# Layer 3 of a graph network: keys and values gathered together, values kept in DRAM in item order

## Chip, cores and metric

The kernel runs on one core of a Trainium2 chip. The time is device microseconds of one execution. Three runs of the kernel before gave 3381.06, 3384.52 and 3429.43 us; the median is 3384.52 us. An engine is named as in the profile: PE is TensorE (PEld its weight loads), DVE VectorE, ACT ScalarE, POOL GpSimd and SP SyncE, which here only issues transfers.

## The reference

Three graph layers run one after the other over 3125 nodes of 256 numbers and 50,000 edges sorted by their destination: two attention convolutions (8 heads, then 1), and one layer of query, key and value attention with 4 heads of 64. Only the third is touched by the change:

```
Q = (enh @ Wq + bq);  K = (enh @ Wk + bk);  V = (enh @ Wv + bv)      # enh = x + 0.1 * query_emb
scores = sum_d Q[dst] * (K[src] + 0.2 * rel[type]) / 8               # per edge and head
w   = exp(scores - max over dst) / (sum over dst)
agg = segment_sum(w * V[src], dst);  msgs = agg where a node has edges, else V
out = layernorm(x + layernorm(msgs @ Wo + bo + x) * gamma + beta)
```

So each edge needs two rows of its source node, one of K for the score and, once all scores are known, one of V for the sum.

## The kernel before

The nodes lie in 25 blocks of 128. The edges are cut into 416 **items** (`ITEMS`): up to 128 edges, one per partition, all of whose destinations lie in one block. Eight items are a **group** (`GROUP`), so there are 52 groups; four groups (`SLOTS`) are a turn (`TURNS` is 13). All engines follow one written program, stage by stage: node1, score1, sum1, node2, score2, soft2, sum2, node3, score3, soft3, sum3, final. A stage begins when the engines it names have ended the one before (`begin`, L345). Otherwise engines meet only in semaphores.

**node3** (`node3_products` L1071, `kv_copies` L1234) makes Q, K and V block by block. Q goes to `query`, a view of the second half of `row_space` in SBUF. K and V go through `stage` to the DRAM tables `tab_k` and `tab_v` with 256 numbers per row, two stores per block (`store`, L502).

**Gathers.** POOL fetches rows by index (`gathers`, L693). One indirect DMA fetches one row for each of the 128 edges of an item, 1 KB each, so a group takes eight of them into one slot (`row_slots`, L165). The pass for K (n = 2) has a ring of four slots, because `query` takes the rest of the space; the pass for V (n = 3) has eight (`RINGS`, L49). Before it fills a slot POOL waits until DVE has read what was in it (`slot_used`, L718). The V pass starts once the K pass is issued, takes its first four slots as they come free, and the other four once PE has ended score3 (L715).

**score3** (`pair_scores` L847 on PE, L1245 on ACT, L1562 on DVE; `score_rows` L526 on SP). For each group SP broadcasts two rows of small numbers to all partitions (types, destinations; 128 KB each as written, in pieces of 1 KB). ACT makes one-hot matrices of them, PE multiplies these with the relations and with Q of the block in two halves of four items, and tells with `pair_mm` that a half is done. DVE waits for the group's K rows and for the half, adds (L1580), multiplies (L1588) and reduces (L1570). ACT's next one-hots wait for `pair_mm` too.

**soft3** normalises the scores with a scan over all edges (L1616).

**sum3** (`sums`, L905 on PE, L1176 on ACT, L1668 on DVE). Per group DVE waits until PE has used the buffer two groups back (`sum_mm`, L1682), builds the one-hot of destinations (L1683), waits for the V rows, weighs them (L1688) and copies the shares (L1692). PE adds the eight items into the PSUM bank of their block (L918) and tells `sum_mm`; ACT moves each full block to `acc` (L1195), which waits for `sum_mm` as well. The same functions make sum2, with rows of layer 2.

**final** reads V back (`load_v`, L497) and makes the output.

`acc` holds the sums of a layer; node3 is the last to read those of layer 2, and sum3 writes it next.

Of the kernel before, what the change touches and what calls it, by code (L numbers as in the profile page):

```python
# [48 lines left out]
RINGS = [2 * SLOTS, 2 * SLOTS, SLOTS, 2 * SLOTS]  # L49
BTURNS = BLOCKS // UB  # L50
# [46 lines left out]
def graph_layers(nc, a, out):  # L97
    ctx = ExitStack()
    with ctx:
# [12 lines left out]
        tab_k = dram("tab_k", (NP, D))  # L112
        tab_v = dram("tab_v", (NP, D))
# [37 lines left out]
        query = query_space[:, 0:BLOCKS * D].rearrange("p (b d) -> p b d", b=BLOCKS)  # L151
# [158 lines left out]
        gathered = [sem(f"rows_gathered{s}") for s in range(2 * SLOTS)]  # L310

# [105 lines left out]
        def _(sp):  # L417
# [79 lines left out]
            def load_v(t, j):  # L497
                if not early(t, j, UB):
                    sp.wait_ge(x_used, nth_block(t, j, 1, 1 - UB))
                sp.dma_start(stage[:, j, 1], tab_v[bass.ds((t * UB + j) * P, P), :]).then_inc(x_loaded[j], 16)  # L500
# [25 lines left out]
            def score_rows(layer, name, first):  # L526
# [7 lines left out]
                with nc.sync.Fori(0, TURNS) as u:  # L534
                    for s in range(SLOTS):

                        sp.wait_ge(onehot_made[s % 2], nth(u, s) + (layer * HALF + 1))
                        for k in range(2):
                            row = flat[k][bass.ds(u * (STEP * P // 2) + s * GROUP * P // 2, GROUP * P // 2)]
                            sp.dma_start(bcast_words[:, s % 2, k], row.partition_broadcast(P)).then_inc(bcast_in[s % 2], 16)  # L540
                end()
# [63 lines left out]
            seg_rows("soft3", H3, P // H3)  # L605

# [20 lines left out]
            stored(5 * BTURNS)  # L627

        @block.gpsimd
        def _(pool):  # L630
# [62 lines left out]
            def gathers(n, table, name):  # L693

                ring, turns, rest = RINGS[n], (GROUPS - 1) // RINGS[n], (GROUPS - 1) % RINGS[n] + 1
                pool.wait_ge(phase["sp"], STAGES.index(name) + 1)

                def indices(u, s):

                    for k in (s, s + 1):  # L700

                        pool.wait_ge(gathered[k], u * (16 * GROUP) + (uses(n, k) * 16 * GROUP))
                    nc.gpsimd.tensor_copy(  # L703
                        index_slot[:, s:s + 2].rearrange("p s g -> p (s g)"),
                        src_i[:, bass.ds(u * (ring * GROUP) + s * GROUP, 2 * GROUP)]).then_inc(pool_step, 1)

                def gather(u, s, ends):
# [12 lines left out]
                    pool.sem_inc(slot_claimed, 1)  # L720
                    for g in range(GROUP):
                        nc.gpsimd.indirect_dma_start(  # L722
                            (wide_rows[:, s] if n == 0 else row_slots[s])[:, g, :], None, table,
                            bass.IndirectOffsetOnAxis(ap=index_slot[:, s, g:g + 1], axis=0),
                        ).then_inc(gathered[s], 16)

                indices(0, 0)
                with nc.gpsimd.Fori(0, turns) as u:
                    for s in range(ring):
                        gather(u, s, False)  # L730
                for s in range(rest):
                    gather(turns, s, s + 1 == rest)
                step.add(GROUPS // 2)
# [3 lines left out]
            gathers(2, tab_k, "node3")  # L737
            gathers(3, tab_v, "node3")
# [365 lines left out]
        def _(act):  # L1104
# [129 lines left out]
            def kv_copies(t, j):  # L1234
                act.wait_ge(node_mm, nth_block(t, j, 2, 1))
                act.wait_ge(node_stored[j], t * 32 + 16 * 2 * BTURNS)
# [40 lines left out]
        def _(dve):  # L1277
# [284 lines left out]
            def pair_scores(layer, name):  # L1562
# [10 lines left out]
                def multiply(u, s, reduce_before):  # L1573
# [3 lines left out]
                    for half in range(2):  # L1577
# [4 lines left out]
                            rows[:, s, items, :].rearrange("p i (h d) -> p i h d", h=H3),  # L1582
# [85 lines left out]
            def sums(n, name, heads, width, nth_pass):  # L1668
# [7 lines left out]
                def build(u, s):  # L1676
# [10 lines left out]
                    dve.wait_ge(gathered[s], u * (16 * GROUP) + ((uses(nth_pass, s) + 1) * 16 * GROUP))  # L1687
# [400 lines left out]
            def final_iteration(t, j):  # L2088
# [63 lines left out]
                if outer_too:  # L2152
                    after(1)

                    dve.wait_ge(node_stored[jd], td * 16 + 16 * 4 * BTURNS)
# [50 lines left out]
```

## Time and profile before

| | us |
|---|---|
| median of three runs | 3384.52 (3381.06 to 3429.43) |
| span of the profiled execution | 3410.9 |
| of it score3, about 1958 to 2645 | 687 |
| soft3, 2645 to 2697 | 52 |
| sum3, 2697 to 3295 | 598 |
| busy PE / DVE / POOL / ACT, whole span | 1633.6 / 1540.5 / 1641.8 / 406.0 |

The profile gives the profiled execution's span alone and no further time around it; 3410.9 us is 26.4 us above the median of the runs and inside their spread. No engine is busy for even half of the span: POOL and PE 48%, DVE 45%. The page's chain of work that ended last puts 36% down to "another core or an unknown queue". The queue of POOL's gathers moved 219.91 MB and took 22.7% of what 16 DMA engines have, SP's queue 69.66 MB and 8.1%. A busy share is an average over stages with different limits, so it has to be read stage by stage.

### The profile page before, as it was taken

Reading aid. Unit: us, or ns where it says so; the run is one execution under the profiler, and the core shown is the slowest. Engines: PE = TensorE matmul, PEld = TensorE weight load, DVE = VectorE, ACT = ScalarE, POOL = GpSimd, SP = SyncE. Lnnn points to the kernel's source line nnn. Section 1 sums busy time; section 2 is a strip of 40 time slices with the busy share of each in tenths; the row PEclk is TensorE's granted clock in tenths of the full one; section 3 lists DMA queues with packets and bytes.
Section 4 is the critical chain, followed back from the end, with each engine's and each line's share of the span. In section 5 each row is a group of like instructions: output and inputs, shape, how many; then the busy total and the mean of one; then the engine's idle time right before and its main releaser. Section 6 shows DMA issues by size and latency. Waiting matters only on the chain.

```text
span 3410.9 us, 30471 instructions
## 1 busy us (share of the span) xinstructions
PE 1633.6 (48%) x7573; PEld 1176.0 (34%) x7574; DVE 1540.5 (45%) x2386; ACT 406.0 (12%) x809; POOL 1641.8 (48%) x1791
## 2 busy tenths in 40 slices
PE   3624334335367342443345945655566233333455
PEld 2313323223255332332233434444344222322343
DVE  3225454536464772232235535545565432322368
ACT  0100000000012000000001433333333100000012
POOL 0240656455502715655660065665656756556600
PEclk8855767667688556766667967777777566666765
DMA  1532323223303522322321343343333323223211
GB/s 33 125 92 55 86 70 92 63 82 82 80 29 99 165 77 83 91 82 82 89 85 34 98 115 98 104 106 98 105 99 102 99 79 91 82 82 89 85 29 61
DMA packets 166449, 289.97 MB, mean 85 GB/s; under 512 B 37842, under 2 KB 113035, under 8 KB 166411
## 3 DMA queue, kind: packets, MB, share of 16 engines
q0 software_dynamic: 79872, 219.91, 22.7%
q1 hardware_dynamic: 86539, 69.66, 8.1%
q14 instruction: 27, 0.22, 0.0%
q8 instruction: 11, 0.18, 0.0%
HBM read 272.74 MB, written 16.68 MB: 85 GB/s over the span
## 4 chain that ended last, share of the span: by engine, by line
another core or an unknown queue 36%; DVE 23%; PE 21%; issue 13%; DMA 4%; DVEq 1%; SPq 1%; ACT 0%; POOL 0%; ACTq 0%; POOLq 0%
PE ps L918 5%; DVE arena L1688 5%; PE ps L870 3%; DMA arena<-rows_block_dst 3%; DVE arena L1931 2%; PE ps L1077 2%; DVE arena L1580 2%; DVE scores L1570 2%; DVE arena L1588 1%; PE ps L797 1%; PE ps L1054 1%; PE ps L1003 1%; DVE arena L1924 1%; DVE arena L1498 1%
## 5 line engine op out<-in xcount | busy, mean ns | idle before, releaser
L722 POOL DMA_INDIRECT row_space<-tab_feat,index_slot x832 | 816.5, 981 | 687.4 <-issue 322.5
L918 PE MATMUL ps<-arena 128*128 128x257 f32 (+1 forms) x1664 | 481.9, 457 | 702.2 <-DVE arena L1692 504.8
L918 PEld LDWEIGHTS ps<-arena 128*128 128x128 f32 x1664 | 379.3, 233 | 804.7 <-issue 731.6
L722 POOL DMA_INDIRECT row_space<-tab_k,index_slot x416 | 393.9, 947 | 255.8 <-issue 162.1
L722 POOL DMA_INDIRECT row_space<-tab_v,index_slot x416 | 403.4, 970 | 229.1 <-issue 128.4
L1683 DVE TENSOR_TENSOR arena<-ps,block_dst 128x1024 f32<-128x1024 f32 x104 | 127.0, 1222 | 809.0 <-remote 681.9
L1003 PE MATMUL ps<-arena 128*128 128x265 f32 x832 | 249.8, 463 | 102.8 <-DVE ps L1914 49.5
L870 PE MATMUL ps<-row_space,arena 128*128 x832 | 294.0, 514 | 0.0
L1580 DVE TENSOR_TENSOR arena<-row_space,ps 128x1024 f32<-128x1024 f32 x104 | 126.8, 1219 | 322.0 <-remote 223.7
L1195 ACT COPY acc<-ps 128x265 f32<-128x265 f32 (+2 forms) x75 | 28.2, 376 | 1786.8 <-remote 1064.6
L1003 PEld LDWEIGHTS ps<-arena 128*128 128x128 f32 x832 | 189.1, 233 | 149.0 <-issue 107.9
L1688 DVE TENSOR_TENSOR arena<-row_space,ps 128x2048 f32<-128x2048 f32 x104 | 236.8, 2277 | 0.0
L703 POOL COPY index_slot<-src_i 128x16 int32 (+1 forms) x104 | 23.8, 229 | 432.8 <-SPq L419 432.5
L864 PE MATMUL ps<-rel_stack,arena 128*128 128x64 bf16 x416 | 92.4, 222 | 275.1 <-DVE arena L1588 159.8
L870 PEld LDWEIGHTS ps<-row_space,arena 128*128 128x128 f32 x832 | 202.1, 255 | 40.0
L864 PEld LDWEIGHTS ps<-rel_stack,arena 128*128 128x128 bf16 x416 | 43.1, 104 | 322.8 <-DVE arena L1588 179.2
L1588 DVE TENSOR_TENSOR arena<-arena,ps 128x1024 f32<-128x1024 f32 x104 | 127.0, 1221 | 9.6 <-DVE arena L1580 3.7
L1570 DVE TENSOR_REDUCE scores<-arena 128x2048 f32 (+1 forms) x52 | 118.5, 2280 | 0.0
L1931 DVE TENSOR_TENSOR arena<-row_space,ps 128x2048 f32<-128x2048 f32 x52 | 118.3, 2276 | 0.0
L950 PE MATMUL ps<-er_parts,arena 128*128 x416 | 56.4, 199 | 127.7 <-issue 74.5
L1253 ACT ACTIVATE arena<-arena,minus_type_no 128x1024 bf16<-128x1024 uint8 x52 | 59.7, 1148 | 446.1 <-remote 332.4
L836 PE MATMUL ps<-el_parts,arena 128*128 128x25 bf16 x1248 | 62.0, 183 | 89.1 <-DVE arena L1498 72.3
(316 smaller groups left out, 2120.1 us busy)
## 6 DMA issues: line engine op xcount, KB each, us to landing
arena<-rows_block_dst SPq DMA_DIRECT2D x156, 128.0 KB
row_space<-tab_feat,index_slot POOLq DMA_INDIRECT x832
arena<-rows_src_low SPq DMA_DIRECT2D x52, 128.0 KB
arena<-rows_type SPq DMA_DIRECT2D x52, 128.0 KB
row_space<-tab_k,index_slot POOLq DMA_INDIRECT x416
row_space<-tab_v,index_slot POOLq DMA_INDIRECT x416
arena<-in_x_t SPq DMA_DIRECT2D x50, 128.0 KB, 2.2
tab_feat<-arena SPq DMA_DIRECT2D x25, 132.0 KB, 1.8
```

The costliest lines, as they stand in the source:

```text
L722: nc.gpsimd.indirect_dma_start((wide_rows[:, s] if n == 0 else row_slots[s])[:, g, :], None, table, bass.IndirectOffsetOnAxis(ap=index_slo ...
L864: nc.tensor.matmul(relation, type_onehot[:, s % 2, e], rel_stack[:, 0, :], start=True, stop=False)
L870: last = nc.tensor.matmul(ps[:, bank, at:at + D], query_onehot[:, s % 2, g * P:(g + 1) * P], query[:, bass.ds(bs[g], 1), :].rearrange("p a ...
L918: last = nc.tensor.matmul(ps[:, SUM_BANKS:2 * SUM_BANKS][:, bass.ds(bs[g], 1), 0:width].rearrange("p a d -> p (a d)"), onehot[:, s % 2, g, ...
L1003: last = nc.tensor.matmul(ps[:, SUM_BANKS:2 * SUM_BANKS][:, bass.ds(banks[s % 2 * GROUP + g], 1), 0:AW].rearrange("p a d -> p (a d)"), one ...
L1077: nc.tensor.matmul(at, h_t[:, j, k, :], w_a[:, k, w0:w1], start=k == 0, stop=False)
L1570: vec.tensor_reduce(by_item(H3)[:, bass.ds(u * STEP + s * GROUP, GROUP), :], pair_product[:, s % 2].rearrange("p i (h d) -> p i h d", h=H3 ...
L1580: then(vec.tensor_tensor(pair_product[:, z, items, :].rearrange("p i (h d) -> p i h d", h=H3), rows[:, s, items, :].rearrange("p i (h d) - ...
L1588: vec.tensor_tensor(pair_product[:, z, items, :], pair_product[:, z, items, :], ps[:, 2 * half:2 * half + 2, :].rearrange("p q (i d) -> p ...
L1683: vec.tensor_tensor(onehot[:, z], ps[:, SHARE_BANK:SHARE_BANK + 1, IOTA_AT:IOTA_AT + P].broadcast_to([P, GROUP, P]), block_dst[:, bass.ds( ...
L1688: vec.tensor_tensor(weighted[:, z, :, 0:D].rearrange("p i (h d) -> p i h d", h=heads), row_slots[s].rearrange("p i (h d) -> p i h d", h=he ...
L1931: vec.tensor_tensor(weighted[:, z, :, 0:D].rearrange("p i (h d) -> p i h d", h=H1), wide_rows[:, half * SLOTS + g, :, 0:D].rearrange("p i ...
```

## The change

- node3 stores K and V of a block as one row of 512 numbers in `tab_kv`, in one store per block.
- Q no longer lies in `row_space` but in `acc`, so that four slots of double width fit (`kv_rows`).
- The K pass gathers from `tab_kv`: as many indirect DMAs as before, with rows of 2 KB. Before it fills a slot again POOL also waits for `values_stored`.
- In score3 SP stores the value half of each group, once gathered, in `item_v`, a DRAM tensor in item order (1 MB per group). It issues that after the next group's broadcasts.
- The V pass of gathers is gone. SP loads the groups of `item_v` plainly into eight slots, the first eight after it has issued soft3's rows, the others in sum3 as DVE frees the slots. DVE waits for `values_in`.

The diff, cut to its core:

```diff
+PREFETCH = 2 * SLOTS
-        tab_k = dram("tab_k", (NP, D))
-        tab_v = dram("tab_v", (NP, D))
+        tab_kv = dram("tab_kv", (NP, 2 * D))
+        item_v = dram("item_v", (GROUPS, P, GROUP * D))
-        query = query_space[:, 0:BLOCKS * D].rearrange("p (b d) -> p b d", b=BLOCKS)
+        kv_rows = row_space[:, 0:SLOTS * GROUP * 2 * D].rearrange("p (s g d) -> p s g d", s=SLOTS, g=GROUP)
+        query = acc[:, :, 0:D]
...
+            def store_values(u, s):
+                sp.wait_ge(gathered[s], u * (16 * GROUP) + (uses(2, s) + 1) * 16 * GROUP)
+                sp.dma_start(item_v[bass.ds(u * SLOTS + s, 1)].rearrange("a p (g d) -> (a p) g d", g=GROUP),
+                             kv_rows[:, s, :, D:2 * D]).then_inc(values_stored[s], 16)
+
+            def load_values(u, s):
+                sp.wait_ge(slot_used[s], u + (uses(3, s) + 1))
+                sp.dma_start(row_slots[s].rearrange("p g d -> p (g d)"),
+                             item_v[bass.ds(u * PREFETCH + s, 1)].rearrange("a p d -> (a p) d")).then_inc(values_in[s], 16)
...
+                else:
+                    spread(0, 0)
+                    with nc.sync.Fori(0, TURNS - 1) as u:
+                        for s in range(SLOTS):
+                            spread(u + (s + 1) // SLOTS, (s + 1) % SLOTS)
+                            keep(u, s)
...
-            pipeline(nc.sync.Fori, [(0, load_x), (4, store(2, tab_k, tab_v))])
-            stored(4 * BTURNS)
+            def store_kv(t, j):
+                sp.wait_ge(node_act, nth_block(t, j, 2, 1))
+                sp.dma_start(tab_kv[bass.ds((t * UB + j) * P, P), :],
+                             stage[:, j].rearrange("p a d -> p (a d)")).then_inc(node_stored[j], 16)
+            pipeline(nc.sync.Fori, [(0, load_x), (4, store_kv)])
...
-            score_rows(2, "score3", "type")
+            score_rows(2, "score3", "type", keep=store_values)
             seg_rows("soft3", H3, P // H3)
+            for s in range(SLOTS):
+                sp.wait_ge(values_stored[s], 16 * TURNS)
+            for s in range(PREFETCH):
+                load_values(0, s)
             begin(sp, "sum3", ["dve", "pe", "act"])
...
+            with nc.sync.Fori(0, GROUPS // PREFETCH - 1) as u:
+                for s in range(PREFETCH):
+                    load_values(u + 1, s)
+            for s in range(GROUPS % PREFETCH):
+                load_values(GROUPS // PREFETCH, s)
...
-                    if n == 3 and s == SLOTS:
-                        pool.wait_ge(phase["pe"], STAGES.index("score3") + 1)
                     pool.wait_ge(slot_used[s], u + (uses(n, s) + 1))
+                    if kept:
+                        pool.wait_ge(values_stored[s], u * 16)
...
-            gathers(2, tab_k, "node3")
-            gathers(3, tab_v, "node3")
+            gathers(2, tab_kv, "node3")
...
-                            rows[:, s, items, :].rearrange("p i (h d) -> p i h d", h=H3),
+                            kv_rows[:, s, items, 0:D].rearrange("p i (h d) -> p i h d", h=H3),
...
-                    dve.wait_ge(gathered[s], u * (16 * GROUP) + ((uses(nth_pass, s) + 1) * 16 * GROUP))
+                    if nth_pass == 3:
+                        dve.wait_ge(values_in[s], u * 16 + 16)
+                    else:
+                        dve.wait_ge(gathered[s], u * (16 * GROUP) + ((uses(nth_pass, s) + 1) * 16 * GROUP))
```

`spread` is the old body of SP's loop, the two broadcasts of one group.

## Rows read from the trace of the kernel before

**Rows 1.** Busy time of the engines by stretch, with PEclk, DMA share and GB/s.
```profile
core 0: us, PE busy (x) PEld busy (x) DVE busy (x) ACT busy (x) POOL busy (x), PEclk, DMA share, GB/s
1112.00:1180.00 68.00, 28.01 (x736) 25.86 (x736) 52.48 (x94) 0.00 (x0) 56.34 (x43) 0.50 0.61 168
1845.00:1935.00 90.00, 76.44 (x241) 35.30 (x241) 59.58 (x181) 35.31 (x124) 0.00 (x0) 0.89 0.29 90
1958.00:2645.00 687.00, 409.80 (x1664) 285.62 (x1664) 362.05 (x257) 227.37 (x208) 420.46 (x466) 0.71 0.39 103
2645.00:2697.00 52.00, 8.96 (x38) 7.06 (x38) 26.75 (x39) 10.89 (x19) 38.32 (x33) 0.53 0.32 91
2697.00:3295.00 598.00, 240.09 (x832) 188.29 (x832) 183.68 (x165) 17.68 (x46) 348.63 (x386) 0.70 0.28 80
3256.00:3292.00 36.00, 31.62 (x128) 25.44 (x128) 27.07 (x25) 4.58 (x12) 0.00 (x0) 0.89 0.00 0
```

**Rows 2.** Groups of instructions in the sum stage of layer 3, 2697 to 3295 us.
```profile
L722 POOL DMA_INDIRECT row_space<-tab_v,index_slot x364 | 344.6, 947 | 204.2 <-issue 112.9 <-DVE arena L1688 89.5 <-POOL index_slot L703 1.8
L1688 DVE TENSOR_TENSOR arena<-row_space,ps 128x2048 f32<-128x2048 f32 x52 | 118.4, 2277 | 0.0
L1683 DVE TENSOR_TENSOR arena<-ps,block_dst 128x1024 f32<-128x1024 f32 x52 | 63.5, 1222 | 412.1 <-remote 359.9 <-PE ps L918 41.2 <-issue 8.4
```

**Rows 3.** Timeline of one cycle of four groups in that stage (start, duration).
```profile
2962.39 0.94 POOL L722 DMA_INDIRECT row_space<-tab_v,index_slot  x1 [9.54 <-DVE arena L1688]
...
2972.09 3.77 PE L918 MATMUL ps<-arena 128*128 128x260 f32 x16 [0.41 <-DVE arena L1692]
...
3001.34 0.95 POOL L722 DMA_INDIRECT row_space<-tab_v,index_slot  x1 [0.30 <-issue]
...
3007.53 0.38 ACT L1195 COPY acc<-ps 128x260 f32<-128x260 f32 x1 [40.93 <-remote]
3007.64 1.22 DVE L1683 TENSOR_TENSOR arena<-ps,block_dst 128x1024 f32<-128x1024 f32 x1 [23.85 <-remote]
```

**Rows 4.** Timeline of its last groups, after the last gather.
```profile
3272.81 1.22 DVE L1683 TENSOR_TENSOR arena<-ps,block_dst 128x1024 f32<-128x1024 f32 x1 [0.55 <-PE ps L918]
...
3276.58 7.28 PE L918 MATMUL ps<-arena 128*128 128x260 f32 x32 [0.30 <-DVE arena L1692]
...
3280.39 1.23 DVE L1683 TENSOR_TENSOR arena<-ps,block_dst 128x1024 f32<-128x1024 f32 x1 [0.55 <-PE ps L918]
...
3291.99 0.21 DVE L1704 TENSOR_SCALAR arena<-acc 128x100 f32<-128x100 f32 x1 [4.57 <-ACTq L1114]
```

**Rows 5.** Timeline of the score stage of layer 1, around its last prefetching gather.
```profile
207.25 0.36 DVE L1737 TENSOR_REDUCE scores<-ps 128x192 f32 x1 [20.05 <-remote]
...
223.23 0.95 POOL L722 DMA_INDIRECT row_space<-tab_feat,index_slot  x1 [0.30 <-issue]
...
228.94 0.36 DVE L1737 TENSOR_REDUCE scores<-ps 128x192 f32 x1 [20.67 <-remote]
```

**Rows 6.** Groups of instructions in the score stage of layer 3, 1958 to 2645 us.
```profile
L722 POOL DMA_INDIRECT row_space<-tab_k,index_slot x416 | 393.9, 947 | 255.8 <-issue 162.1 <-DVEq L1301 91.8 <-POOL index_slot L703 1.5
L1580 DVE TENSOR_TENSOR arena<-row_space,ps 128x1024 f32<-128x1024 f32 x103 | 125.6, 1219 | 316.0 <-remote 217.8 <-issue 65.9 <-PE ps L870 29.1
```

**Rows 7.** Timeline of one cycle of two groups in that stage.
```profile
2310.58 0.94 POOL L722 DMA_INDIRECT row_space<-tab_k,index_slot  x1 [6.07 <-DVEq L1301]
...
2328.41 1.22 DVE L1580 TENSOR_TENSOR arena<-row_space,ps 128x1024 f32<-128x1024 f32 x1 [9.66 <-remote]
...
2335.55 0.95 POOL L722 DMA_INDIRECT row_space<-tab_k,index_slot  x1 [5.19 <-issue]
...
2354.03 1.22 DVE L1580 TENSOR_TENSOR arena<-row_space,ps 128x1024 f32<-128x1024 f32 x1 [10.66 <-remote]
```

**Rows 8.** Stretches as in Rows 1: broadcasts alone; gathers and broadcasts together.
```profile
231.00:319.00 88.00, 46.15 (x340) 35.55 (x339) 44.94 (x87) 0.00 (x0) 0.00 (x0) 0.50 0.28 61
2346.00:2348.00 2.00, 1.11 (x3) 0.34 (x1) 0.00 (x0) 0.00 (x0) 1.51 (x2) 0.50 0.86 109
```

More of the change, by code:

```diff
@@ L310, in graph_layers @@
         gathered = [sem(f"rows_gathered{s}") for s in range(2 * SLOTS)]
+        values_stored = [sem(f"values_stored{s}") for s in range(SLOTS)]
+        values_in = [sem(f"values_loaded{s}") for s in range(2 * SLOTS)]
         slot_claimed = sem("rows_slot_claimed")
@@ L499, in load_v @@
                     sp.wait_ge(x_used, nth_block(t, j, 1, 1 - UB))
-                sp.dma_start(stage[:, j, 1], tab_v[bass.ds((t * UB + j) * P, P), :]).then_inc(x_loaded[j], 16)
+                sp.dma_start(stage[:, j, 1], tab_kv[bass.ds((t * UB + j) * P, P), D:2 * D]).then_inc(x_loaded[j], 16)
             def store(stage_no, *tables):
@@ L524, in _, with score_rows @@
             end()
-            def score_rows(layer, name, first):
+            def store_values(u, s):
[6 more added lines that the diff above has]
+                             item_v[bass.ds(u * PREFETCH + s, 1)].rearrange("a p d -> (a p) d")).then_inc(values_in[s], 16)
+            def score_rows(layer, name, first, keep=None):
                 begin(sp, name, ["dve", "pe", "act"])
@@ L533, in score_rows, with spread @@
                 flat = [rows_d[x].rearrange("i e -> (i e)") for x in (first, "block_dst")]
-                with nc.sync.Fori(0, TURNS) as u:
+                def spread(u, s):
+                    sp.wait_ge(onehot_made[s % 2], nth(u, s) + (layer * HALF + 1))
+                    for k in range(2):
+                        row = flat[k][bass.ds(u * (STEP * P // 2) + s * GROUP * P // 2, GROUP * P // 2)]
+                        sp.dma_start(bcast_words[:, s % 2, k], row.partition_broadcast(P)).then_inc(bcast_in[s % 2], 16)
+                if keep is None:
+                    with nc.sync.Fori(0, TURNS) as u:
+                        for s in range(SLOTS):
+                            spread(u, s)
+                else:
[4 more added lines that the diff above has]
+                            keep(u, s)
                     for s in range(SLOTS):
[L537 to L540, printed above, removed]
+                        if s + 1 < SLOTS:
+                            spread(TURNS - 1, s + 1)
+                        keep(TURNS - 1, s)
                 end()
@@ L600, in _ @@
                 sp.dma_start(bias_parts[k:k + 1, :], bias_split[:, k]).then_inc(bias_in, 16)
-            pipeline(nc.sync.Fori, [(0, load_x), (4, store(2, tab_k, tab_v))])
-            stored(4 * BTURNS)
+            def store_kv(t, j):
[3 more added lines that the diff above has]
+            pipeline(nc.sync.Fori, [(0, load_x), (4, store_kv)])
+            stored(3 * BTURNS)
             end()
-            score_rows(2, "score3", "type")
+            score_rows(2, "score3", "type", keep=store_values)
             seg_rows("soft3", H3, P // H3)
+            for s in range(SLOTS):
+                sp.wait_ge(values_stored[s], 16 * TURNS)
+            for s in range(PREFETCH):
+                load_values(0, s)
             begin(sp, "sum3", ["dve", "pe", "act"])
@@ L626, in _ @@
             pipeline(nc.sync.Fori, [(0, load_v), (5, store_out)])
-            stored(5 * BTURNS)
+            stored(4 * BTURNS)
         @block.gpsimd
@@ L705, in indices, with gather @@
                         src_i[:, bass.ds(u * (ring * GROUP) + s * GROUP, 2 * GROUP)]).then_inc(pool_step, 1)
-                def gather(u, s, ends):
+                rows_of_slot = {0: lambda s: wide_rows[:, s], 1: lambda s: row_slots[s], 2: lambda s: kv_rows[:, s]}[n]
+                def gather(u, s, ends, kept=False):
                     if s % 2 == 0:
@@ L727, in gathers @@
                 indices(0, 0)
-                with nc.gpsimd.Fori(0, turns) as u:
+                if n == 2:
                     for s in range(ring):
-                        gather(u, s, False)
+                        gather(0, s, False)
+                    with nc.gpsimd.Fori(0, turns - 1) as u:
+                        for s in range(ring):
+                            gather(u + 1, s, False, True)
+                else:
+                    with nc.gpsimd.Fori(0, turns) as u:
+                        for s in range(ring):
+                            gather(u, s, False)
                 for s in range(rest):
-                    gather(turns, s, s + 1 == rest)
+                    gather(turns, s, s + 1 == rest, n == 2)
                 step.add(GROUPS // 2)
@@ L1235, in kv_copies @@
                 act.wait_ge(node_mm, nth_block(t, j, 2, 1))
-                act.wait_ge(node_stored[j], t * 32 + 16 * 2 * BTURNS)
+                act.wait_ge(node_stored[j], t * 16 + 16 * 2 * BTURNS)
                 nc.scalar.copy(stage[:, j, 0, :], ps[:, product_bank(j), D:2 * D])
```

5 lines of the change are left out of this document (3 added, 2 removed).

## The prediction

> **What bounds the kernel now.** I read the page's slices first and saw no engine near full use, so I cut the span by stage [rows 1]. In sum3 (2697 to 3295 us) PE is busy 240 of 598 us, DVE 184, and the DMA engines carry 28% of what they can. POOL has 349 us of gathers, and with the gap after each of them they come every 1.25 us: eight per group and a copy of indices make about 10.1 us, so 52 groups cost POOL some 525 us. Next I read who waits in it: DVE never waits at the weighing that needs the rows (0.0 idle before L1688), but 412 us before the one-hot (L1683), 360 of them with an unknown releaser [rows 2]. By the program that instruction waits for PE's signal alone.
>
> The timeline shows what that is [rows 3]. POOL restarts at 2962.39 when DVE frees slots and issues four groups, 32 gathers, until 3002.29. PE finishes a group of matmuls at 2975.86 (2972.09 plus 3.77), yet ACT and DVE, who both wait for PE's count, move only at 3007.53 and 3007.64: 32 us after the matmuls and 5 us after POOL's last gather. The eight slots then free four again, and so on: 40 us of gathers plus 9.4 is the 49.4 us cycle. The rows themselves were there long before. Two more places bear out that PE's signals come late while POOL issues back to back, and not otherwise. At the end of sum3, with all gathers issued, two groups take 7.58 us (3272.81 to 3280.39), and PE's 7.28 us fill it [rows 4]. In score1, where DVE needs nothing gathered, its reductions stand at 207.25 and 228.94, and the second comes 4.8 us after POOL's last prefetch ended [rows 5]. In the stretch 1112 to 1180 of score2 it does not happen, though gathers and broadcasts move 168 GB/s: there the gathers are slower, 56.34 us for 43, 1.31 us each [rows 1]. I don't know the mechanism; the rows tie it to POOL issuing at full pace, not to bytes moved.
>
> Score3 is the same with four slots: POOL issues two groups (16 gathers, about 20 us), then waits about 5 us for DVE; it starts at 2310.58 and 2335.55, and DVE begins every second group 25.6 us apart [rows 7]. POOL's waits there are 256 us, DVE's 316 [rows 6].
>
> **The change, part by part.**
>
> Sum3 without POOL. The 416 gathers of V go. What is left per group is DVE's 1.22 + 2.28 us beside PE's 3.64 plus its gap, 3.79 in the steady pair [rows 2, 4]. From the start of the stage at 2697 [rows 1] to the first instruction of final at 3291.99 [rows 4] is now 595 us. After: 50 groups × 3.79 = 190, plus the 11.6 us from the one-hot of the last pair (3280.39) to that instruction, plus 3 us for PE starting at 1.2 GHz (granted clock 0.5) before it has 2.4: 204 us. **Gain 391 us.** ACT's copies of blocks already keep up at that pace in the last groups.
>
> The plain loads of V must feed this: 1.05 MB per 3.79 us is 277 GB/s. Eight groups are there before, since SP issues them during soft3 (52 us). The other 44 are 46.1 MB. No row shows 1 MB loads in pieces of 8 KB. Bounds: broadcasts alone carry 61 GB/s at a DMA share of 0.28 [rows 8], that is 218 GB/s, and 46.1 MB take 212 us; node loads and stores carry 90 GB/s at 0.29 [rows 1], 310 GB/s, and 149 us. With eight groups of lead 310 is ample, and 218 makes the stage about 15 us longer. I take no cost: long plain pieces should be nearer the node loads. SP's issues are cheap and in order, and only loads of weights stand ahead of them.
>
> Score3, gathers. The count is 416 as before, and POOL's pace per gather is that of descriptors, not bytes, as far as rows of 1 KB tell: no change of 10.1 us per group. But each moves 2 KB rows. Per pair of groups the DMA engines get 4.19 MB of gathers, 2.10 MB of stores of V and 0.52 MB of broadcasts. From rates at full share: gathers as in sum3, 80 GB/s at 0.28, 286 [rows 1]: 14.7 us. Stores as in node3, 310: 6.8 us. Broadcasts 218: 2.4 us. Sum 23.9 us in a cycle that now has 25.0 (POOL) to 25.6 (DVE). By score3's own mix, 103 GB/s at 0.39 = 264 GB/s, it is 25.8 us. So the stage moves from 39% to full DMA use. Ends: longer rows could be cheaper per byte, and then nothing changes (0); or the mix is dearer, as in the 2 us at 2346, 109 GB/s at a share of 0.86, 127 GB/s [rows 8], 54 us per pair. That end is two microseconds of one burst with small pieces in it, so I stay near the whole stage's mix and add 1 us for what queues at the burst's end: 26.8 us per pair, **24 pairs × 1.8 = +43 us**.
>
> Score3, the new waits. POOL waits also for the slot's store. A group is used by DVE some 30 us after its last gather (the group issued 2310.58 to 2320.3 starts at 2354.03 [rows 7]; its slot cannot be freed sooner). SP stores it when it has landed, a 1 MB store is 3.4 us at 310 GB/s, and even twice that ends long before: 0. If that cover went, the store's 3.4 us and the landing would come on each group. SP's order is the other risk: the store of group k stands before the broadcasts of k+2. Those are wanted only after PE has done group k, which needs DVE at k−1, while the rows of k have landed earlier: 0. ACT and DVE get no new instruction, and reading keys at double stride changes no shape.
>
> Score3's end. POOL's last gather of K is issued four groups before the end, and then the V pass fills the gap in the kernel before. Now POOL is silent, and the last four groups run at PE's 409.8/52 = 7.9 us instead of 687/52 = 13.2 [rows 1]: **−21 us**.
>
> Small edits, together: one 256 KB store instead of two per block in node3 (SP's issues lie beside PE's 76 of 90 us), Q copied to `acc`, the strided load in final: 0. Soft3: its chain is DVE, PE and ACT one after the other, and SP waits for the last stores behind soft3's rows, hidden by 52 us: 0.
>
> Sum: −391 + 43 − 21 = −369 us. Against the profiled 3410.9 us span that is 3042. The profiled execution stands 26.4 us above the median of the runs; carried to the median 3384.5 the forecast is **3015 us**.
>
> **A rule weighed.** The sum takes bytes at the rates of the rows. The Trainium skill, "DMA: Bandwidth & Descriptors", section Measured, lists 6.15 us for a transfer of 1 MB. By it 44 loads take 271 us, and sum3 would be bound by them; no run here shows a plain 1 MB load, and the rows' own lower bound is 218 GB/s. That speaks against this change, and stands below as rival C with its price from rows. The same page says transfers from all issuing engines interleave on the same 16 DMA engines, which the shares above assume and no row of mine separates.
>
> **Rivals.**
>
> A, 20%: score3's stall ends only when the gathers' queue has drained, not when POOL stops. For it: the release comes about 5 us after the last gather [rows 3, 5], time in which a queue could drain. Then the stores' 6.8 us per pair lie on the path, 31.8 instead of 25.0: 26 × 6.8 = 177, less the 21 of the end. Time 3384.5 − 391 + 156 = 3150.
>
> B, 8%: the opposite. Fuller DMA engines slow POOL's issue, as something does in score2 at 1.31 us per gather, and PE's signals come in time [rows 1]. Then score3 is bound by the DMA's 23.9 us per pair: 26 × 23.9 = 621 against 687. Time 3384.5 − 391 − 66 = 2928. Against it: the slowing in score2 goes with DVE's work there, which score3 does not have.
>
> C, 10%: loads bind sum3, which they do from below about 235 GB/s. At 218 GB/s the stage is 15 us longer; the dearest row I have, 127 GB/s [rows 8], makes it 165 longer. I price the middle, 172 GB/s: 268 us for the 44 loads, some 70 longer, time about 3085. Eight slots, and so several loads in flight, speak against it.
>
> D, 6%: signals come late under any heavy transfer, not POOL's. Four loads of 3.7 us and the 9.4 us of overhead of today's cycle [rows 3] give 24.2 us per four groups, 13 × 24.2 = 315 us for sum3. Time 3384.5 − 280 + 22 = 3126. Against it: the 168 GB/s of score2 without such stalls.
>
> E, 4%, slower than before: gathers, stores and broadcasts together fall to the 127 GB/s of the burst row [rows 8]. Then score3 takes 26 × 54 = 1400 us, 713 more, and the kernel 3384.5 − 391 + 713 = 3706. It decides from where a pair costs 25.0 + 391/26 = 40 us, 170 GB/s. The 168 GB/s of score2 at a share of only 0.61 speaks against that.
>
> **Numbers.** The forecast has 52%, with its own range 2960 to 3075. Predicted time 3015. The range 2930 to 3190 takes in A, C and D and half of B; outside it are E, the rest of B and the tails of A and C. A difference of 2%, 68 us, is about what a measurement of this kernel can tell from none. All cases but E lie far beyond it: faster 0.94, within 2% 0.02 (an A and a D together with dear stores), slower 0.04.
>
> **What would show it.** Right: no gathers in sum3, two groups of it about 7.6 us apart throughout, the stage near 205 us, PEclk near 1.0 in it; score3 at 680 to 740 us with a DMA share above 0.85 and POOL's 16 gathers still about 20 us long. Wrong: waits of DVE for `item_v` loads in sum3 (C); one-hots there with unknown releasers (D); POOL's pause in score3 grown from 5 to 12 us (A), or gone (B); gathers visibly longer than 1.25 us apart with the stage far over 750 us (E).

## The result, and the profile after

The changed kernel takes 3006.05 us (median of 4 runs, 2986.95 to 3031.9) against 3385.88 us before (median of 4 runs with one more taken beside it, 3381.06 to 3429.43): a ratio of 0.887, 95% interval 0.883 to 0.891. The forecast was 3015 us. The profiled execution, 3031.9 us, is the slowest of the four and counted as a slow run, while the ratio is of fast runs. Its span is 3030.2 us against 3410.9, 381 us less.

By stretch, in the profiled executions (us):

| | before | after | difference |
|---|---|---|---|
| start to the first gather of score3 | 1957.7 | 1963.0 | +5.3 |
| its 416 gathers, first to last | 654.0 | 676.3 | +22.3 |
| from the last gather to DVE's last product | 40.7 | 23.4 | −17.3 |
| from there over soft3 to the first one-hot of sum3 | 43.7 | 43.0 | −0.7 |
| sum3, to the first instruction of final | 595.9 | 205.3 | −390.6 |
| final | 118.9 | 119.2 | +0.3 |

The stretches after, to set beside [rows 1]: score3, soft3, sum3, the middle of sum3.

```profile
core 0: us, PE busy (x) PEld busy (x) DVE busy (x) ACT busy (x) POOL busy (x), PEclk, DMA share, GB/s
1963.00:2662.00 699.00, 398.20 (x1664) 279.81 (x1664) 363.13 (x259) 227.37 (x208) 399.10 (x441) 0.71 0.78 254
2662.00:2704.00 42.00, 8.95 (x38) 7.04 (x38) 24.06 (x37) 8.67 (x13) 0.00 (x0) 0.54 0.53 210
2704.00:2912.00 208.00, 190.93 (x832) 154.56 (x832) 183.63 (x158) 19.93 (x53) 0.00 (x0) 0.98 0.64 224
2720.00:2900.00 180.00, 170.69 (x752) 138.34 (x751) 164.36 (x141) 16.57 (x43) 0.00 (x0) 1.00 0.69 244
```

In sum3 POOL does nothing, PE is busy 191 of 208 us and its granted clock is 0.98 of full speed, where it was 0.70 in a stage in which PE was busy 240 of 598 us. The groups of that stage, beside [rows 2] (L1735 is the one-hot, L1743 the weighing):

```profile
L970 PE MATMUL ps<-arena 128*128 128x260 f32 x832 | 190.9, 387 | 19.8 <-DVE arena L1747 19.8
L1743 DVE TENSOR_TENSOR arena<-row_space,ps 128x2048 f32<-128x2048 f32 x52 | 118.4, 2277 | 0.0
L1735 DVE TENSOR_TENSOR arena<-ps,block_dst 128x1024 f32<-128x1024 f32 x52 | 63.7, 1224 | 20.7 <-PE ps L970 18.1 <-ACT ps L1233 2.6
```

DVE's wait before the one-hot fell from 412 to 21 us, and none of it has an unknown releaser ("remote") any more. The wait for the loaded values would stand before L1743; it is 0.0. The timeline of the steady stage, beside [rows 4]:

```profile
2799.63 1.22 DVE L1735 TENSOR_TENSOR arena<-ps,block_dst 128x1024 f32<-128x1024 f32 x1 [0.66 <-PE ps L970]
...
2803.14 1.23 DVE L1735 TENSOR_TENSOR arena<-ps,block_dst 128x1024 f32<-128x1024 f32 x1
...
2807.32 1.22 DVE L1735 TENSOR_TENSOR arena<-ps,block_dst 128x1024 f32<-128x1024 f32 x1 [0.66 <-PE ps L970]
```

Two groups take 7.69 us; without any transfer they took 7.58. The transfers of the values, from the page's list of DMA issues (count, KB each, median us from issue to landing where it has one):

```profile
item_v<-row_space SPq DMA_DIRECT2D x52, 1024.0 KB
row_space<-item_v SPq DMA_DIRECT2D x52, 1024.0 KB, 4.8
```

Score3, beside [rows 6] (L1632 is the product with the keys):

```profile
L768 POOL DMA_INDIRECT row_space<-tab_kv,index_slot x416 | 394.0, 947 | 278.0 <-issue 173.5 <-DVEq L1353 103.5 <-POOL index_slot L748 1.0
L1632 DVE TENSOR_TENSOR arena<-row_space,ps 128x1024 f32<-128x1024 f32 x104 | 126.7, 1219 | 327.4 <-remote 284.5 <-PE ps L922 23.0 <-issue 17.8
```

A gather of 2 KB rows costs POOL the same 947 ns as one of 1 KB rows. POOL waits 22 us more than before, DVE 11 us more, still mostly for an unknown releaser, and the DMA engines carry 254 GB/s at a share of 0.78 instead of 103 at 0.39. The gathers of a group take the same 9.80 us from the first issue to the end of the last, before and after; what grew is POOL's 24 pauses for a free slot, from 5.61 to 6.55 us on average, 22.6 us together.

The trace also records when a semaphore is raised, and that tells whose signal is late. From the end of a PE instruction that signals to the next recorded raise of its semaphore it takes 6.03 us in the median in this score3, where the same figure for DVE's and for ACT's signals is 0.01 us. In sum3 it was 6.74 us for PE before the change, up to 3240 us; it was 0.01 us there after the last gather, and it is 0.01 us after the change. (Where signals queue up the next raise can belong to an earlier one, and some raises are not recorded, so the figures of late signals are rough.)

### The profile page after: what moved, and what is told of

Same layout as the page of the kernel before. It is cut to its first block, busy times and chain, and to the rows that moved or that the text cites. A ratio compares the mean times of both kernels' runs of the same rounds, so it can differ in the third digit from the quotient of the medians.

```text
span 3030.2 us, 30129 instructions
## 1 busy us (share of the span) xinstructions
PE 1576.3 (52%) x7573; PEld 1138.0 (38%) x7574; DVE 1541.8 (51%) x2386; ACT 406.2 (13%) x809; POOL 1228.8 (41%) x1349
## 4 chain that ended last, share of the span: by engine, by line
another core or an unknown queue 28%; PE 27%; DVE 24%; issue 14%; DMA 5%; DVEq 1%; SPq 1%; ACT 0%; POOL 0%; ACTq 0%; POOLq 0%
PE ps L970 7%; DVE arena L1743 5%; PE ps L922 5%; DMA arena<-rows_block_dst 4%; PE ps L1129 2%; DVE arena L1986 2%; PE ps L1055 2%; DVE arena L1632 2%; PE ps L849 2%; PE ps L1106 1%; DVE scores L1622 1%; DVE arena L1979 1%; DVE arena L1640 1%; DVE arena L1550 1%
## 5 line engine op out<-in xcount | busy, mean ns | idle before, releaser
L970 PE MATMUL ps<-arena 128*128 128x257 f32 (+1 forms) x1664 | 427.4, 419 | 364.2 <-DVE arena L1747 305.7
L970 PEld LDWEIGHTS ps<-arena 128*128 128x128 f32 x1664 | 341.7, 210 | 449.9 <-issue 389.4
L768 POOL DMA_INDIRECT row_space<-tab_kv,index_slot x416 | 394.0, 947 | 278.0 <-issue 173.5
L1735 DVE TENSOR_TENSOR arena<-ps,block_dst 128x1024 f32<-128x1024 f32 x104 | 127.2, 1223 | 415.7 <-remote 327.9
L1632 DVE TENSOR_TENSOR arena<-row_space,ps 128x1024 f32<-128x1024 f32 x104 | 126.7, 1219 | 327.4 <-remote 284.5
L922 PE MATMUL ps<-acc,arena 128*128 x832 | 285.4, 502 | 0.0
L1055 PEld LDWEIGHTS ps<-arena 128*128 128x128 f32 x832 | 191.5, 236 | 149.6 <-issue 107.5
L1743 DVE TENSOR_TENSOR arena<-row_space,ps 128x2048 f32<-128x2048 f32 x104 | 236.8, 2277 | 0.0
L922 PEld LDWEIGHTS ps<-acc,arena 128*128 128x128 f32 x832 | 197.4, 249 | 38.6
L888 PEld LDWEIGHTS ps<-el_parts,arena 128*128 128x128 bf16 x1248 | 57.7, 108 | 105.1 <-issue 57.6
```

The costliest lines, as they stand in the source:

```text
L768: nc.gpsimd.indirect_dma_start(rows_of_slot(s)[:, g, :], None, table, bass.IndirectOffsetOnAxis(ap=index_slot[:, s, g:g + 1], axis=0),).th ...
L888: nc.tensor.matmul(ps[:, bank, at:at + w], onehot_t[:, s % 2, 0, e], el_parts[:, k, 0:w], start=k == 0, stop=k == 2)
L922: last = nc.tensor.matmul(ps[:, bank, at:at + D], query_onehot[:, s % 2, g * P:(g + 1) * P], query[:, bass.ds(bs[g], 1), :].rearrange("p a ...
L970: last = nc.tensor.matmul(ps[:, SUM_BANKS:2 * SUM_BANKS][:, bass.ds(bs[g], 1), 0:width].rearrange("p a d -> p (a d)"), onehot[:, s % 2, g, ...
L1055: last = nc.tensor.matmul(ps[:, SUM_BANKS:2 * SUM_BANKS][:, bass.ds(banks[s % 2 * GROUP + g], 1), 0:AW].rearrange("p a d -> p (a d)"), one ...
L1632: then(vec.tensor_tensor(pair_product[:, z, items, :].rearrange("p i (h d) -> p i h d", h=H3), kv_rows[:, s, items, 0:D].rearrange("p i (h ...
```

## The experiments

My theory: TensorE's signals to the other engines come late while POOL issues gathers at full pace. Sum3 was bound by that, and score3 still is. Against it: the stage was bound by the gathers' transfers, or by POOL's own time; and score3's 22 us could come from the longer rows or from the stores. Twelve runs were made, each beside the kernel before on its chip. Experiments 1 to 10 are one execution each. Experiments 1 to 4 ran on one chip, 5 to 10 on a second, 11 and 12 on a third (on which chip the result above was measured is not known); there the kernel before took 3441.6, 3441.6 to 3469.9, and 2809.7 us. Stages are compared within one chip where that can be done.

**1. Gathers nobody needs, in sum3.** The changed kernel, where POOL also issues 144 gathers:

```diff
             gathers(2, tab_kv, "node3")
+            for u in range(12):
+                for k in range(3):
+                    if u: pool.wait_ge(spare_in[k], u * 64)
+                    for g in range(4):
+                        nc.gpsimd.indirect_dma_start(spare[:, k, g, :], None, tab_feat2, ...).then_inc(spare_in[k], 16)
```

> The changed kernel, and in its sum3 POOL issues 144 gathers of layer 2's rows (1 KB each, about 180 us of issuing at 1.25 us each) into spare SBUF; nothing in the kernel waits for them but POOL itself. Theory (PE's signals come late while POOL issues back to back): as in score1, one or two groups per 21 us while POOL runs, so 10 to 17 groups in 180 us instead of 47, then 3.8 us each: sum3 about 320 us instead of 208, the kernel 3090 to 3140 us. Rival 1 (sum3 was slow because its rows came from POOL): no wait is added, sum3 stays 205 to 215 us, the kernel 2985 to 3030. Rival 2 (the bytes matter): 144 x 128 KB = 19 MB more in 180 us lifts the DMA share from 0.65 to about 1.0, sum3 up by 10 to 30 us.

Measured: 3259.38 us, sum3 381.4 us instead of 205.3. POOL's gathers span 2757.5 to 2937.8 us. Groups in 2757 to 2938, then DVE's one-hots and PE's products in the timeline:

```profile
L801 POOL DMA_INDIRECT scores<-tab_feat,index_slot x144 | 136.6, 949 | 115.6 <-ACT ps L1249 72.0 <-issue 43.6
L1751 DVE TENSOR_TENSOR arena<-ps,block_dst 128x1024 f32<-128x1024 f32 x7 | 8.6, 1224 | 161.2 <-remote 114.1 <-issue 44.5 <-ACT ps L1249 2.6
L1759 DVE TENSOR_TENSOR arena<-row_space,ps 128x2048 f32<-128x2048 f32 x7 | 15.9, 2278 | 0.0
```

```profile
2770.99 3.77 PE L986 MATMUL ps<-arena 128*128 128x260 f32 x16 [0.41 <-issue]
...
2802.10 1.23 DVE L1751 TENSOR_TENSOR arena<-ps,block_dst 128x1024 f32<-128x1024 f32 x1 [31.36 <-remote]
...
2847.01 1.23 DVE L1751 TENSOR_TENSOR arena<-ps,block_dst 128x1024 f32<-128x1024 f32 x1 [41.39 <-remote]
```

While POOL issues, a group takes 44.9 us (2802.10 to 2847.01, then 2891.87 and 2936.70); when it stops, 3.84. The one-hot at 2847.01 waits for PE's products of two groups back, and these end at 2774.76 (2770.99 plus 3.77). Their signal is sent 72 us before it counts: the semaphore is raised at 2801.97, at 2825.12 and then at 2846.88, one signal after the other. DVE uses nothing that these gathers bring, and the loaded values are there on time (0.0 before L1759), so neither data nor the loads hold the stage: the issues do, with the transfers they start. PE signals twice in a group, once per four items, which makes 22.4 us for each signal; score1 before the change, with one per group, had 21.7 [rows 5]. That is harsher than I had expected: I had priced the end of a burst, and it is a rate of one signal to some 18 issues.

**2. The same with a register load on POOL after each gather**, 108 gathers, to slow their pace:

```diff
+                        pool.load([spare_reg], order_flag[0:1, 0:1])
```

> As the run with 144 idle gathers in sum3, but 108 of them, each followed by a register load from SBUF on POOL, so that they come some 1.6 to 2 us apart and last as long (about 180 to 215 us). If back-to-back issuing is what delays PE's signals: sum3 stays near 208 us (under 230), the kernel 2985 to 3040. If any gather by POOL delays them, in proportion to gathers: 108/144 of the loss of the other run. If the register load itself delays signals, as much as the other run or more.

Measured: 3232.65 us, sum3 335.3. The load did not slow the issues (108 in 134.7 us, 1.25 us each), so it tests no pace. It gives a second size: the loss is 130 us against 176, a ratio of 0.74 where the counts have 0.75. At this pace the loss goes by the number of issues, or by the time that they last.

**3. No stores of V in score3** (POOL's wait for them goes too); sum3 loads rows of `tab_kv` instead, so the sums are of other values:

```diff
-                sp.dma_start(item_v[...], kv_rows[:, s, :, D:2 * D]).then_inc(values_stored[s], 16)
+                sp.sem_inc(values_stored[s], 16)
```

> The changed kernel without the 52 stores of values to item_v in score3 (SP only counts them as done), and the loads of sum3 read rows of tab_kv in place of item_v, 1 MB each in pieces of 8 KB as before; the values summed are therefore other ones. Theory (the stores cost score3 through DMA bandwidth): score3 from first to last gather falls from 676 us back to about 654, its DMA share from 0.79 to about 0.55. Rival (the double rows cost it): stays near 676. Either: sum3 unchanged at 208 us.

Measured: 3040.02 us. Score3's gathers took 660.2 us; in experiments 1 and 2, on the same chip with the same score3 as the changed kernel, 690.4 and 693.8. The DMA share of the stage was 0.61 (expected: 0.55). So the stores cost some 30 us there. That is enough for all of the 22 us, though the run does not tell the stores' bytes from POOL's wait for them. What the rows of 2 KB cost it cannot say: the 654.0 of before is from another execution, and the changed kernel's gathers took 676.3 us there and 690.4 on this chip.

**4. A register load after each gather of score3.**

```diff
+                        if n == 2: pool.load([pause_reg], order_flag[0:1, 0:1])
```

> The changed kernel with a register load from SBUF on POOL after each gather of score3, so that they are 1.5 to 2 us apart. If pace is what delays PE's signals, POOL's 52 x 8 x 1.6 us = 665 us becomes the bound and the unknown waits of DVE and ACT (284 and 306 us) shrink to under 100 us; score3 is then 52 x 8 x the new pace, and shorter than 699 us if the pace is under 1.65 us. If not, the stalls stay and score3 grows by at least 416 x 0.3 = 125 us.

Measured: 3068.2 us, gathers 701.2 us, again at 1.25 us each within a burst. Inconclusive on pace, for the reason of number 2.

**5. Spare gathers in sum3 with two one-column operations of POOL after each**, 108 of them:

```diff
+                        nc.gpsimd.tensor_copy(pause_col[:, at:at + 1], iota_free[:, 0:1])
+                        nc.gpsimd.iota(pause_col[:, 128 + at:129 + at], [[0, 1]], base=0, channel_multiplier=1, ...)
```

> The changed kernel, and in sum3 GpSimd also issues 108 gathers (1 KB rows of tab_feat2 into a part of scores that is free by then, nobody reads them), each followed by two one-column operations of GpSimd itself (a tensor_copy and an iota), so that between two issues GpSimd runs something else. Without those two operations 144 such gathers took sum3 from 205 to 381 us, with one group per 44.8 us while they were issued. If TensorE's signals are held up by a number of issues (some 18 of them to a signal, whatever stands between), 108 gathers cost 108/144 of 176 us = 132 us: sum3 335 to 340 us, one group per 36 issues. If a signal passes as soon as GpSimd leaves the issuing for its own operation, sum3 stays near 205 to 215 us.

Measured: 3109.35 us, sum3 288.9: a loss of 83 us, between the two expectations. The gathers come every 1.43 us, and from 2728.18 to 2839.66 eleven groups take 10.1 us each, where it was 44.9 at 1.25 us. From a PE instruction to the next raise of its semaphore it is 2.69 us in the median over these groups. In the stretch of score2 before the change [rows 1] it was 1.30 and 1.89 us for its two semaphores, with 40 gathers 1.69 us apart. (The 1.31 us that the prediction compares with 1.25 is POOL's busy time divided by 43 instructions, three of them copies of indices; a gather there was busy 1.35 us, against 0.95.) So the delay shrinks as the issues come further apart. Neither pure form of the theory holds: it is not a fixed number of issues per signal, and a short gap does not let every signal pass.

**6. Spare gathers in fours, POOL waiting for the landing of each four**, 72 of them:

```diff
+                    pool.wait_ge(spare_in[k], (u + 1) * 64)
```

> The changed kernel, and in sum3 GpSimd also issues 72 of the same gathers, but after every four it waits until these four have landed before it issues the next four, so that it is silent for some us between fours. If TensorE's signals are held up only while issues follow on one another, they pass in each silence: with a silence per four issues (some 5 us of issuing and 2 us of silence), a group takes at most two such rounds, 14 us, against 44.8 back to back, and sum3 is at most 205 + 18 rounds x 7 us x (1 - 3.84/14) = 297 us, and near 215 us if each silence passes every signal that stands. If the hold-up goes by the number of issues, 72 gathers cost 72/144 of 176 us = 88 us, sum3 293 us, with 36 issues per group. The rate of groups while they are issued tells the two apart: 14 us or less, or 60 us and more.

Measured: 3022.52 us, sum3 206.0. Groups in 2700 to 2860, within the 167.6 us of the gathers:

```profile
L801 POOL DMA_INDIRECT scores<-tab_feat,index_slot x66 | 62.5, 947 | 97.8 <-DMA scores<-tab_feat,index_slot 82.6 <-issue 15.2
L1752 DVE TENSOR_TENSOR arena<-ps,block_dst 128x1024 f32<-128x1024 f32 x42 | 51.4, 1225 | 16.2 <-PE ps L987 16.0
```

With silences of about 5 us after every four, the same gathers cost nothing, and DVE's unknown releasers are gone. It is issues that follow closely on one another, not gathers as such. Nor is it how full the DMA engines are, as the same view shows for experiment 1 and then for this one:

```profile
2767.00:2937.00 170.00, 24.20 (x81) 18.48 (x79) 14.39 (x13) 0.00 (x0) 128.52 (x137) 0.60 0.44 134
2700.00:2860.00 160.00, 151.79 (x660) 122.76 (x659) 143.83 (x124) 11.57 (x30) 62.40 (x66) 0.99 0.89 323
```

The signals came late at a DMA share of 0.44 and 134 GB/s, and in time at 0.89 and 323 GB/s. What no run separates is the issuing itself from the packets that dense gathers put in flight.

**7. One one-column copy of POOL after each gather of score3.**

```diff
+                        if n == 2: nc.gpsimd.tensor_copy(pause_col[:, ...], iota_free[:, 0:1])
```

> The changed kernel, with one more one-column operation of GpSimd after each of the 416 gathers of score3. At 0.1 to 0.3 us each they add 40 to 120 us to GpSimd's own time. If score3 is bound by signals that wait for GpSimd's issues to end, and each such operation lets them pass, score3 gets shorter than the changed kernel's on this chip (by as much as the 173 us that GpSimd itself waits there beside its issues allow). If it is bound by GpSimd's issues, or the signals do not pass in so short a pause, score3 gets longer by 20 to 100 us.

**8. The changed kernel itself**, on the same chip.

> The changed kernel itself, beside the others on their chip, for the stages of score3 on the same chip: sum3 205 us, score3 between 700 and 720 us, whole kernel 3010 to 3070 us.

Measured: 2992.03 us with the copies, 2993.67 without; from the first gather of score3 to the last product 679.3 against 699.5 us. The groups of POOL in that stage, with the copies and then without:

```profile
L769 POOL DMA_INDIRECT row_space<-tab_kv,index_slot x416 | 403.7, 970 | 157.9 <-DVEq L1356 92.2 <-issue 64.5 <-POOL index_slot L749 0.8
L774 POOL COPY pause_col<-iota_free 128x1 f32 (+1 forms) x415 | 80.5, 194 | 2.6 <-issue 0.2
```

```profile
L768 POOL DMA_INDIRECT row_space<-tab_kv,index_slot x416 | 393.9, 947 | 273.3 <-issue 205.0 <-DVEq L1353 67.3 <-POOL index_slot L748 1.0
```

Number 8 has sum3 at 205.6 us as expected, and the kernel's time lies below the 3010 to 3070 expected. POOL does 80 us more with the copies, and the stage is 20 us shorter, since it waits 115 us less; the unchanged score3 of experiments 5, 6 and 8 took 700.2, 695.8 and 699.5 us on this chip. So score3 is bound by the late signals, not by POOL's own time. The kernel's time does not show it: the stages before score3 took 18.6 us longer in that execution.

**9 and 10. Two copies after each gather in score3, or five together after each eight**; in layer 2 one after every second, or four after every four; in layer 1 one after each, or five after each eight.

```diff
+PACE = {0: (1, 1, 0), 1: (1, 2, 416), 2: (2, 1, 624)}
...
+                        ops, every, at = PACE[n]
+                        if g % every == every - 1:
+                            for i in range(ops):
+                                nc.gpsimd.tensor_copy(pause_col[:, ...], iota_free[:, 0:1])
```

This is number 9; number 10 has `{0: (5, 8, 0), 1: (4, 4, 260), 2: (5, 8, 676)}`. The three numbers of a layer are how many copies, after how many gathers, and where they write.

> The changed kernel with one-column copies of GpSimd (about 0.15 to 0.2 us each) between its gathers: one after each gather in layer 1, one after every second gather in layer 2, two after each gather in score3. One copy after each gather took score3 from 699.5 to 679.3 us and GpSimd's own time to 1.325 us per gather. Two make about 1.47 us per gather, 12.0 us per group, 624 us for the 52 groups. If what holds TensorE's signals is a queue that GpSimd fills at full pace and that empties in any gap, score3 comes down to 635 to 665 us, GpSimd hardly waiting any more; if it goes by the number of issues, score3 is 720 us or more. In sum2 (570.7 us, 12.3 us per group once the prefetched ones are used up) one copy to two gathers makes 10.7 us per group on GpSimd: 530 to 560 us if signals gain by it, 575 to 590 if not.

> The changed kernel with GpSimd's silences gathered together: five one-column copies (some 0.9 us) after each group of eight gathers in layer 1 and in score3, four (some 0.7 us) after every four gathers in layer 2. GpSimd's own time is some 11.1 us per group, 577 us for score3. If one silence of a microsecond lets every waiting signal of TensorE pass, score3 is 590 to 640 us and sum2 520 to 550 us. If a signal needs a gap between all issues, or silences of some microseconds as where GpSimd waits for landings, score3 stays at 680 us or more, and sum2 at 570 us or more.

Measured: 2996.63 and 3020.24 us. Score3 672.0 and 712.4 us, against 699.5; the one-hots of sum2 span 572.0 and 561.2, against 570.7. A gap after each issue helps in score3, a silence of under 1 us after every eight issues does not (it costs 13 us). Sum2 gains 9.5 us by pauses after every four. Score3 with two copies and both values of sum2 lie between the branches that I had named; all of it is less than I had expected.

**11. The spacings that gained, together**, and **12. the changed kernel again**, timed in several rounds on one chip:

```diff
+PACE = {0: (0, 8, 0), 1: (4, 4, 0), 2: (2, 1, 416)}
```

> The changed kernel with the two spacings of GpSimd's gathers that gained in single looks: in layer 2 four one-column copies after every four gathers (sum2 561 instead of 571 us), in score3 two after each gather (672 instead of 699.5 us); layer 1 as it is. The two gains add up to 37 us, 1.2% of the kernel: 0.012 below the changed kernel's ratio on the same chip, where sum1, which differs by 20 us from run to run of the same code, does not blur it. If the looks misled, the two ratios agree within 0.003.

> The changed kernel itself, timed beside the spaced one on the same chip: the ratio to the kernel before is the one measured first, 0.87 to 0.89.

Measured: on this chip the kernel before takes 2809.66 us (9 runs), the changed one 2529.38 (5 runs, ratio 0.900, interval 0.899 to 0.901), the spaced one 2642.17 (5 runs, 0.940, 0.939 to 0.942). Both expectations missed. The changed kernel here in score3, sum3 and sum2:

```profile
1621.00:2143.00 522.00, 385.25 (x1626) 272.36 (x1627) 349.32 (x250) 223.03 (x205) 398.47 (x441) 0.79 0.99 334
2200.00:2408.00 208.00, 191.08 (x832) 154.70 (x832) 182.99 (x158) 20.43 (x54) 0.00 (x0) 0.98 0.63 224
1100.00:1480.00 380.00, 218.45 (x600) 166.03 (x599) 132.79 (x114) 15.72 (x41) 290.40 (x322) 0.74 0.36 104
```

and its groups in the first of these stretches:

```profile
L768 POOL DMA_INDIRECT row_space<-tab_kv,index_slot x416 | 394.0, 947 | 124.2 <-issue 120.0 <-DMA row_space<-tab_kv,index_slot 2.1 <-POOL index_slot L748 1.8
L1632 DVE TENSOR_TENSOR arena<-row_space,ps 128x1024 f32<-128x1024 f32 x101 | 122.9, 1217 | 164.8 <-PE ps L922 125.0 <-DMA row_space<-tab_kv,index_slot 38.8 <-DVE arena L1640 0.2
```

The unknown releasers are gone: DVE waits for PE or for data. POOL issues without a break, 10.05 us per group, and its 120 us of "issue" are the 0.3 us after each gather. The signals are not late on this chip, though POOL's pace is the same: from a PE instruction to the raise of its semaphore it is 0.01 us in the median in score3, 0.02 at most. Score3 takes 538.5 us instead of 699.5, sum3 the same 205.4. So spacing only costs here: score3 becomes 610.4 us, sum2's one-hots 475.9 instead of 439.8, together 108 of the 113 us. What differs between the chips no trace shows.

The gain of the change is 280 us on this chip, 380 in the result above, and 448 by the one execution of each on the second chip (3441.6 against 2993.67). The kernel before has no trace here. An estimate: its sum3 would go at POOL's 10.1 us for the 44 groups that were not there ahead, 445 us, and some 12 at its end as in [rows 4], so that 205 in its place gives about 250; where the other 30 came from was not traced.

## Why the prediction was right, step by step

- **Sum3 without POOL, −391: measured −390.6.** The stage was forecast at 204 us and is 205.3. Experiments 1, 2 and 6 show the cause: the same stage takes 44.9 us per group while POOL issues without a pause, and 3.8 us with POOL silent in between. (Before the change POOL had a pause per four groups, and a group took 49.4/4 = 12.4 us. One group did pass within the burst of [rows 3], with a one-hot at 2980.27.) The pair of the last groups [rows 4] was the right row to price it by.
- **The loads of V, no cost: right.** DVE never waits for them (0.0 before L1743). The bounds were 218 and 310 GB/s at a full share; the trace has 244 at a share of 0.69, 354 at full. Rival C is refuted. The 6.15 us for 1 MB in the Trainium skill ("DMA: Bandwidth & Descriptors", section Measured) does not bind here: 4.8 us from issue to landing with one or two loads in flight, and the first eight, issued together, had landed 22.9 us after the first issue, 366 GB/s.
- **Score3's gathers, +43: measured +22.** This is the term that was mis-sized, and its reason was wrong. I took the stage to become bound by the DMA engines, 26.8 us per pair of groups. They were at 0.78 of full use instead, where I had named a share above 0.85 as a sign of being right. On the last chip the same bytes went in 20.1 us per pair (522/26) at a share of 0.99, 334 GB/s against the 264 of the old mix (in the result above 254 GB/s at 0.78, or 326 at full use): the mix with rows of 2 KB and stores is cheaper per byte. Experiment 3 puts the 22 us on the stores, and they lie in POOL's pauses (24 of 6.55 us instead of 5.61), not in its gathers; how the stores lengthen the pauses stays open. On the last chip they show no cost: all of POOL's waits for transfers are 2.1 us.
- **Score3's end, −21: measured −17.** The end of the stage shrank from 40.7 to 23.4 us; that this is because no pass of V follows fits the theory and was not tested by itself.
- **The new waits, node3's store, soft3, final: 0.** Soft3 −0.7, final +0.3. What comes ahead of score3 is +5.3, less than the same code differs by on one chip (first gather of score3 at 1924.8 us in experiment 8, 1957.5 in 5 and in 6, all on the second chip).
- **Rivals.** A: POOL's waits in score3 grew by 22 us (278.0 against 255.8 [rows 6]), not by 177; refuted as a whole, though the stores' 22 to 30 us may be a small form of it. B did not happen in the result above or on the first two chips, but on the last one the signals come in time, and score3 is 538.5 us, below even B's 621: not because POOL is slowed, as B said, since its gathers are 947 ns there too. B's premise had the reading of score2 wrong besides (see experiment 5). D: refuted by sum3 at 244 GB/s without a stall. E: refuted, 254 GB/s where it needed under 170.

The forecast of 3042 us for the profiled execution met 3030.2: too dear by 21 in score3, too hopeful by 4 at its end, and 5 elsewhere. That 3015 met the median of 3006.05 as well is partly luck: it was carried over by the 26.4 us by which the profiled execution before lay above its median, and the one after happens to lie 25.9 above its own. The size is also that of the chip: on the third chip the gain is 280 us, where the forecast has 369.

No version was shown to beat the changed kernel. The spaced one is shorter in score3 on one chip and 4.5% slower as a whole on another.

## What to carry to other kernels

When an engine waits for a releaser that the profile cannot name, while its data are there and POOL issues indirect gathers one behind the other, take the gathers out of that stage: rows that were gathered once can be kept in item order and loaded plainly. That cost the loading stage nothing here, and the stores cost the gathering stage some 22 to 30 us (on the third chip they show no cost). Price such a stage by the few groups that run after the last gather. Try a spacing of the issues on more than one chip before you keep it: what won 20 to 27 us of a stage on one lost 72 on another.

## What the runs showed of the hardware that I had not expected

- While POOL issued gathers every 1.25 us, PE's signals passed at one in 22.4 us (experiment 1), 18 issues to a signal, and queued: one was 72 us late. DVE's and ACT's own signals were in time (0.01 us in the median, score3 after the change). At 1.43 us per gather a group with two signals took 10.1 us (experiment 5); with 5 us of silence after every four gathers nothing was lost (experiment 6), at a DMA share of 0.89, twice the 0.44 of experiment 1.
- It differs between chips: on the last one the same program has no such waits, at the same 947 ns per gather, and takes 2529 instead of 2994 us.
- A register load between POOL's gathers does not slow them: 1.25 us each with and without it (experiments 2 and 4).
- A gather of 128 rows of 2 KB costs POOL the same 947 ns as one of 1 KB rows, and with stores and broadcasts beside it the DMA engines moved 334 GB/s at a share of 0.99.
